# A graph convolution's first edge layer as two 64-row products in two PSUM banks, with the row numbers in SBUF

## The reference

```
h = silu(edge_scalars @ fc_w1 / sqrt(8)) * SILU_NORM      # 8 numbers per edge -> 64
w = h @ fc_w2 / sqrt(64)                                  # 64 -> 4 * 64 weights per edge
xg0, xg1 = y0[edge_src], y1[edge_src]                     # rows of the source node
mid0 = w_a * xg0 * ea0 ; mid1 = w_b * einsum(xg1, ea1)
mid2 = w_c * xg0 * ea1 ; mid3 = w_d * ea0 * xg1
agg = segment_sum([mid0, mid1, mid2, mid3], edge_dst)     # then two more linear layers, layer norm
```

## Time and profile before

| | |
|---|---|
| median of 3 runs | 4439.98 us (4437.06 to 4447.93) |
| the profiled execution | 4438.43 us, of which the span of the program's instructions is 4437.0 us |
| busy: PE, DVE, POOL, ACT | 3977.1, 3643.9, 3236.4, 1558.8 us |
| edge loop of the convolution (first to last gather starts) | 86.6 to 2214.8 us |
| attention | from about 2285 us to the end |

### The profile page before, as it was taken

How to read it: one execution, slowest core, us unless ns; L and a number is a source line. 1 busy time by engine, 2 the same in 40 slices (tenths; PEclk the granted TensorE clock), 3 DMA queues, 4 the chain that set the end, 5 groups by cost and what they waited for, 6 DMA issues and landing times. The chain is left out here.

```text
span 4437.0 us, 108028 instructions
## 1 busy us (share of the span) xinstructions
PE 3977.1 (90%) x29492; PEld 2525.2 (57%) x29492; DVE 3643.9 (82%) x10493; ACT 1558.8 (35%) x3201; POOL 3236.4 (73%) x3375
## 2 busy tenths in 40 slices
PE   6899999999999999999958999899999989899897
PEld 5444444444444444444446766676667667667665
DVE  2888888888888888888838888888888888888887
ACT  4222222222222222222213444444444444444444
POOL 3777777777777777777727777777777777777774
PEclk8999999999999999999968888888888888888888
DMA  7667676666766667666644444444444444444443
GB/s 276 192 201 210 195 210 200 201 207 194 209 200 204 204 194 212 197 205 203 195 133 122 123 124 124 123 123 125 123 123 125 124 123 123 123 126 124 123 126 85
DMA packets 443567, 727.04 MB, mean 164 GB/s; under 512 B 147552, under 2 KB 279666, under 8 KB 443492
## 3 DMA queue, kind: packets, MB, share of 16 engines
q0 software_dynamic: 160832, 443.98, 37.1%
q1 hardware_dynamic: 282660, 282.22, 19.7%
HBM read 578.28 MB, written 147.55 MB: 164 GB/s over the span
## 5 line engine op out<-in xcount | busy, mean ns | idle before, releaser
L993 POOL DMA_INDIRECT sub_xg<-y_rows,sub_meta x1662 | 1618.6, 974 | 574.0 <-issue 435.3
L2326 POOL DMA_INDIRECT ord_xg<-xpa_rows,ord_meta x1666 | 1597.0, 959 | 511.5 <-issue 467.3
L2394 PE MATMUL ord_a<-ord_xg,ord_sel 128*128 128x264 f32 x3332 | 1139.6, 477 | 118.8 <-DVE ord_xg L2757 118.0
L1044 PE MATMUL sub_a<-sub_mids,sub_sel 128*32 128x128 f32 x13296 | 902.6, 308 | 176.5 <-DVE sub_mids L1333 173.9
L2394 PEld LDWEIGHTS ord_a<-ord_xg,ord_sel 128*128 128x128 f32 x3332 | 720.4, 238 | 257.2 <-DVE ord_xg L2757 130.7
L1333 DVE TENSOR_TENSOR sub_mids<-sub_w,sub_xg 128x384 f32<-128x384 f32 x1662 | 839.6, 546 | 0.0
L1044 PEld LDWEIGHTS sub_a<-sub_mids,sub_sel 128*32 128x32 f32 x13296 | 406.7, 110 | 596.7 <-DVE sub_mids L1333 313.6
L1328 DVE TENSOR_TENSOR sub_mids<-sub_w,sub_xg 128x256 f32<-128x256 f32 x831 | 349.2, 420 | 307.4 <-DMA sub_xg<-y_rows,sub_meta 228.9
L1024 PE MATMUL sub_w<-sub_fc,sub_ht 64*128 64x256 f32 x3324 | 591.7, 433 | 0.0
L2757 DVE TENSOR_TENSOR ord_xg<-ord_xg,ord_prob 128x1024 f32<-128x1024 f32 x476 | 510.0, 1071 | 0.2 <-issue 0.2
L1313 DVE SCALAR_TENSOR_TENSOR sub_sel<-sub_dve,sub_rel,sub_meta 128x128 f32<-128x128 f32 x1668 | 498.5, 340 | 0.0
(11 more groups left out here) (201 smaller groups left out, 4054.2 us busy)
## 6 DMA issues: line engine op xcount, KB each, us to landing
sub_sum_rows<-sub_zeros SPq DMA_DIRECT2D x554, 80.0 KB
sub_sum_rows<-sub_agg_s SPq DMA_DIRECT2D x554, 64.0 KB
sub_node_rows<-sub_sum_rows SPq DMA_DIRECT2D x49, 640.0 KB, 5.5
sub_loop_odds<-sub_sum_rows SPq DMA_DIRECT2D x46, 640.0 KB
ord_xg<-xpa_rows,ord_meta POOLq DMA_INDIRECT x1666
sub_xg<-y_rows,sub_meta POOLq DMA_INDIRECT x1662
ord_x_rows<-x_rows SPq DMA_DIRECT2D x119, 128.0 KB
out_dram<-ord_res SPq DMA_DIRECT2D x119, 128.0 KB
```

What stands on the lines that cost most here:

```text
L993: nc.gpsimd.indirect_dma_start(xg[:, b, k], None, y, bass.IndirectOffsetOnAxis(ids[:, b, 0, k:k + 1], 0))\
L1044: mm = nc.tensor.matmul(a[ROWS * m:ROWS * (m + 1), 0:w].rearrange("p (q f) -> p q f", f=MUL), sel[:, b, k, m], of, start=(j == 0), stop=(j ...
L2326: nc.gpsimd.indirect_dma_start(xg[:, b, k], None, xpa, bass.IndirectOffsetOnAxis(ids[:, b, k:k + 1], 0))\
L2394: mm = nc.tensor.matmul(psum_a[b % 2][:, 0:WIDE], sel[:, b, k], xg[:, b, k], start=(k == 0), stop=(k == TILES - 1 and not has(i, b, -1)), ...
```

## The change

The first layer of half a group becomes two products of 192 columns. The first half of the columns (`r = 0`) has its operands on partitions 0 to 63, the second (`r = 1`) on partitions 64 to 127, so they use the two 64-row tiles of TensorE, and each writes its own PSUM bank. The edge scalars come in two transfers in place of one, to partitions 0 to 15 and 64 to 79, and the small weight `fc_w1` goes to four places in place of two. The second bank is won by taking away the copy of the row numbers in PSUM: `select` reads them from SBUF.

```
-        es = ph.sb("es", [P, SUB_TURN, PAIRS * P])
+        QUARTER = PAIRS * P // 4
+        es = ph.sb("es", [P, SUB_TURN, 2, QUARTER])
...
-        psum_h = ph.ps("h", [P, 512])
+        psum_h2 = ph.ps("h", [P, 2, 512])
+        psum_h = psum_h2[:, 0]
...
-        psum_own = ph.ps("dve", [P, 512])
-        ramp = psum_own[:, 0:ROWS]
+        ramp = c["ramp"][:, 0:ROWS]
...
-                    sp.dma_start(es[0:2 * SCALARS, b], io["sub_scalars_t"][:, bass.ds(g * PAIRS * P, PAIRS * P)])\
-                        .then_inc(meta_in[b], 16)
+                    scalars = io["sub_scalars_t"][:, bass.ds(g * PAIRS * P, PAIRS * P)]\
+                        .rearrange("f (q r x) -> r f q x", q=2, r=2)
+                    for r in range(2):
+                        sp.dma_start(es[MUL * r:MUL * r + 2 * SCALARS, b], scalars[r]).then_inc(meta_in[b], 16)
...
-                        sp.dma_start(fc1[h * SCALARS:(h + 1) * SCALARS, h * MUL:(h + 1) * MUL], io["fc_w1"])\
-                            .then_inc(weights_in, 16)
+                        for r in range(2):
+                            at = MUL * r + h * SCALARS
+                            sp.dma_start(fc1[at:at + SCALARS, h * MUL:(h + 1) * MUL], io["fc_w1"])\
+                                .then_inc(weights_in, 16)
...
-                    part = slice(q * HALF_PAIRS * P, (q + 1) * HALF_PAIRS * P)
-                    nc.tensor.matmul(psum_h[:, 0:HALF_PAIRS * P], fc1[:], es[:, b, part], start=True,
-                                     stop=True).then_inc(h_done, 1)
+                    for r in range(2):
+                        part = slice(r * MUL, (r + 1) * MUL)
+                        mm = nc.tensor.matmul(psum_h2[:, r, 0:QUARTER], fc1[part], es[part, b, q], start=True,
+                                              stop=True, skip_group_check=True)
+                    mm.then_inc(h_done, 1)
...
-                                         psum_h[:, 0:HALF_PAIRS * P], ACT.Silu, scale=1.0 / math.sqrt(SCALARS))\
+                                         .rearrange("f (r x) -> f r x", r=2),
+                                         psum_h2[:, :, 0:QUARTER], ACT.Silu, scale=1.0 / math.sqrt(SCALARS))\
...
-                nc.vector.tensor_copy(ramp, c["ramp"][:, 0:ROWS]).then_inc(set_up, 1)
```

More of the change, by code:

```diff
@@ L797, in convolve_in_order @@
         proj_a = ph.sb("proj_a", [P, 2, 2, 2 * HEADS])
-        psum_h = ph.ps("h", [P, 512])
+        psum_h2 = ph.ps("h", [P, 2, 512])
+        psum_h = psum_h2[:, 0]
         psum_w = ph.ps("w", [P, 4, 512])
         psum_a = [ph.ps(f"a{b}", [P, 512]) for b in range(2)]
-        psum_own = ph.ps("dve", [P, 512])
-        ramp = psum_own[:, 0:ROWS]
+        ramp = c["ramp"][:, 0:ROWS]
         zeroed, weights_in, scaled = ph.sem("zeroed"), ph.sem("weights_in"), ph.sem("scaled")
-        set_up = ph.sem("set_up")
         cleared_es = ph.sem("cleared_es")
@@ L986, in turn @@
                             break
-                        wait_alone(pool, meta_in[b], 32 * (i + 1))
+                        wait_alone(pool, meta_in[b], 48 * (i + 1))
                         for k in range(tiles_of(g)):
@@ L1006, in hidden @@
                     if q == 0:
-                        pe.wait_ge(meta_in[b], 32 * (i + 1))
+                        pe.wait_ge(meta_in[b], 48 * (i + 1))
                     if not (first and q == 0):
                         pe.wait_ge(silu_done, 2 * g + q)
-                    part = slice(q * HALF_PAIRS * P, (q + 1) * HALF_PAIRS * P)
-                    nc.tensor.matmul(psum_h[:, 0:HALF_PAIRS * P], fc1[:], es[:, b, part], start=True,
-                                     stop=True).then_inc(h_done, 1)
+                    for r in range(2):
[3 more added lines that the diff above has]
+                    mm.then_inc(h_done, 1)
                 def weigh(g, b, u, early):
@@ L1127, in turn @@
                         pe.wait_ge(zeroed, 4)
-                        pe.wait_ge(weights_in, 16 * 8)
+                        pe.wait_ge(weights_in, 16 * 10)
                         hidden(0, 0, 0, 0, True)
@@ L1186, in silu @@
                         act.wait_ge(w_done, PAIRS * (g - SUB_TURN + 1))
-                    nc.scalar.activation(ht[:, b, q * HALF_PAIRS:(q + 1) * HALF_PAIRS].rearrange("f u p -> f (u p)"),
-                                         psum_h[:, 0:HALF_PAIRS * P], ACT.Silu, scale=1.0 / math.sqrt(SCALARS))\
+                    nc.scalar.activation(ht[:, b, q * HALF_PAIRS:(q + 1) * HALF_PAIRS].rearrange("f u p -> f (u p)")
+                                         .rearrange("f (r x) -> f r x", r=2),
+                                         psum_h2[:, :, 0:QUARTER], ACT.Silu, scale=1.0 / math.sqrt(SCALARS))\
                         .then_inc(silu_done, 1)
@@ L1286, in _ @@
                     nc.vector.memset(psum_a[b][:], 0.0).then_inc(zeroed, 1)
-                nc.vector.tensor_copy(ramp, c["ramp"][:, 0:ROWS]).then_inc(set_up, 1)
-                dve.wait_ge(weights_in, 16 * 8)
+                dve.wait_ge(weights_in, 16 * 10)
                 nc.vector.tensor_scalar(fc2[:], fc2[:], SILU_NORM / math.sqrt(MUL), None,
@@ L1294, in _ @@
                                         ALU.mult).then_inc(scaled, 1)
-                dve.wait_ge(set_up, 1)
                 def place(g, b, i):
-                    dve.wait_ge(meta_in[b], 32 * (i + 1))
+                    dve.wait_ge(meta_in[b], 48 * (i + 1))
                     shape = [P, GROUP_SUBS, RUN]
```

## The result

The changed kernel takes 4461.56 us in the median of five runs (4456.2 to 4465.29), against 4440.85 (4437.06 to 4447.93) of five runs of the kernel before beside them. The ratio is 1.004 with an interval from 1.003 to 1.0051: slower, by 20.7 us between the medians. The forecast was 4452, 12.5 us more than before. The profiled execution took 4461.56 us, its span is 4460.1.

A forecast was written before the change was run, and what follows sets the result against it. POOL's unbroken row of gathers was taken to bound the loop. select's hold, 11.5 us, plus 1 us at the loop start gave 12.5 us on 4438.43, so 4451; runs' median 1.5 higher, forecast 4452 us, range 4440 to 4471.

The forecast's parts named there:

- POOL bounds the loop, and TensorE's saving is worth nothing: Edge loop: POOL's unbroken row of gathers sets the length, so 86 us less on TensorE gains nothing.
- TensorE sets the pace after all: Rival, edge loop: late sums make POOL stand, so TensorE's saving brings 4354 us at most; chance 0.04.
- The hold of a `select` and how often it is met: Edge loop: select with two SBUF tensors delays gathers starting in its hold, 173 of 1668, 0.067 us each.
- No hold: Rival, edge loop: select gets its repeated operands without holding the gather, 4441 us; chance 0.16.
- the whole instruction: Rival, edge loop: select holds gathers for its full 0.34 us, costing 75 us, 4516 us; chance 0.04.
- The choice of 0.133 us: select in the edge loop: hold taken as its streaming time, 128 elements at 1.04 ns each.
- the longer hold: Rival, edge loop: select holds 0.21 us, costing 29 us, gathers' mean up by 17 ns, 4470 us; chance 0.13.
- the term of 11.5 us for `select`: Edge loop: 173 gathers delayed 0.067 us each by select's hold, lengthening the loop by 11.5 us.
- The loop's start: Head of the loop: extra transfers cost 1 us, between 0 and 2.5; the first gather stays at 86.6.
- The gaps on POOL "still at 0.305": Edge loop: POOL's time between gathers stays 0.305 us each, showing that the loop is POOL's.
- Loads and attention: Steady loads: 47 us more of SyncE issues lie in waits and cost nothing; the attention isn't touched.

The follow-up runs named there:

- The row numbers alone: Kernel before with only select's row numbers read from SBUF, the first layer staying one product of 384 columns; 4460.99 us, ratio 1.0039.
- two spread kernels: Fold's addition in four pieces of 320 columns set apart by other VectorE work: 4416.21 us on the kernel before, 4436.71 on the changed kernel.
- `layer_twice`: Kernel before with the second half's first layer computed twice into the same bank; 4476.8 us, ratio 1.0072.
- `fold_first`: Changed kernel with the fold calls ahead of the pair's selects instead of behind them; 4458.54 us, ratio 1.0041.
- five pieces: Kernel before with fold's addition of 1280 elements cut into five of 256, no waits between: 4431.23 us; with waits: 4476.72 us.
- `after_spread`: Changed kernel with fold's addition in four pieces of 320 columns, set apart by other VectorE work; 4436.71 us, ratio 0.9992.

## Why the prediction came out as it did

**POOL bounds the loop, and TensorE's saving is worth nothing: right.** The row numbers alone gave the whole loss, and 90 us less on TensorE changed nothing that can be measured. That the 90 agrees with the 86 of the forecast is luck: a half takes 0.49 us where I had 0.60, so the first layer itself became 118.9 us cheaper, and other work of TensorE took more, with the mean clock of the loop down from 0.99 to 0.96. In the two spread kernels, both at 0.98, TensorE is busy 117.5 us less. The rival "TensorE sets the pace after all" is out. What the step did not say is that this holds in one direction only: `layer_twice` shows that the slack is used up at certain tiles.

**The hold of a `select` and how often it is met: right.** 165 meetings and 11.9 us, against 173 and 11.5. The delay is the time to the VectorE instruction's recorded end, less 0.13, as the earlier trace rows had it. "No hold" and "the whole instruction" are out. The choice of 0.133 us was right too: the hold begins 0.06 to 0.08 us after the start of a `select`, so it is not the longer one of 0.21. The page of the Trainium skill that the prediction drew on ("SBUF — State Buffer", section SBUF: two separate sides) has it that whichever starts first, a VectorE instruction with two SBUF inputs or a GpSimd one, gets the pair for the whole instruction. The 0.13 us by which the hold ends early, the 0.06 us by which it begins late, and the mean of 987 ns disagree.

**What was mis-sized: the term of 11.5 us for `select` in the sum.** It measured about 21. The step took each meeting as one gather waiting for one instruction, with half the hold left on average. But a `select` that holds may stand right ahead of a `fold`, which starts some 0.05 us after the end of its hold, and then the gather can wait for both. Six of 46 turns had it, at 1.5 us each: 9 us. The forecast's own range ended at 4461, and the mean of a gather rose by 13 ns, not 7. This fits my rival of the longer hold (17 ns) about as well as the forecast; only the single rows tell them apart, since a longer hold would have made the meetings more and longer and begun with the `select`. How much of the loss is a handover is no constant: 4.6 us with the row numbers alone (with 4.7 more under folds alone), none with the `fold` first, yet the sum stays at 20 to 21 us in all four kernels that have the change in `select`. I cannot derive that sum from the meetings by chance. It stays open what sets the phase of the selects against the gathers, by which `fold_first` met 235 and the change 165.

**The loop's start: sign wrong, small.** I forecast 1 us of loss, and none of it ahead of the first gather. But from the first `es` issue to that gather are 3.6 to 3.7 us in the three kernels with two transfers and 2.7 to 3.1 in the seven with one; the two issues took 0.81 us and not 2 x 0.34. The issue itself goes out anywhere from 82.3 to 84.8 us, so the 0.74 of one pair of profiles is partly scatter. The two waits in the head are 1.9 shorter together; with the row numbers alone, where the first layers are as before, they are 1.27 and 1.03, so what shortens them stays open.

**The gaps on POOL "still at 0.305": nearly.** Seven late gaps of 2.3 us in all appeared, six of them close behind a stretch at the lower clock. I had not thought of the clock at all. `select` lasts 0.343, not 0.340.

**Loads and attention: right.** SyncE's extra issues cost nothing visible, and the attention's gathers take 958 ns at the mean, with nothing changed there.

Not tried: the two-tile product without the row numbers in SBUF. It needs a PSUM bank that the copy of the row numbers takes.

## What to carry to other kernels

Where one engine's queue never stands still, look inside its instructions for what makes some of them longer, and price an edit by whether it adds to those; a busy share elsewhere is neither a gain to collect nor a reserve to spend. When two engines share something for the length of an instruction, count not only how often they meet but what follows directly behind: back-to-back holders can act as one long holder. Breaking up a long holder pays if other work stands between the pieces (24 us here) and costs if the engine that is broken up becomes late (35 us).

## What the runs showed of the hardware that I had not expected

- **A waiting gather may be passed over.** Behind a `select` with a `fold` that started 0.05 us after the end of its hold, VectorE had it again in 9 of 11 cases (six of six in the changed kernel, three of five with the row numbers alone); between five pieces, as close, in 16 of 39, and a gather that was passed over once then waited for the whole rest of the row in all 16. Between two selects of a pair the gather got in nearly always: the second starts 0.04 us after the end of the first one's hold, but its own begins only 0.06 to 0.08 us later. The exact rule stays open.
- **Hundredths of a microsecond decide who waits.** In the profiles with an undivided `fold`, a gather that started 0.020 or 0.022 us ahead of one ran free (0.96 us), and one that started 0.017 or 0.019 us ahead waited for the whole of it (2.33 us). Four cases fix no limit. In return, a `select` of the changed kernel lasted up to 0.405 us, not 0.34, where a gather started 0.03 to 0.08 us after it and ran free.
- **A lower clock came with less work on TensorE, but not always**: 0.96 in the loop after the change against 0.99 before (0.98 with the row numbers alone), with the second layer at 1.23 us in place of 0.70 in one such stretch. `fold_first` has 0.96 too, but `after_spread`, with the same first layer, 0.98 like the spread kernel without it. What brings the clock down stays open.
